# Output product of a gated slot attention layer: from two exact float32 pairs to twelve products of rounded halves, and two TensorE steps moved

## The reference, cut to what matters

```python
q = short_conv(h @ Wq, cq); k = short_conv(h @ Wk, ck); v = short_conv(h @ Wv, cv)
w = l2norm(short_conv(h @ Ww, cv)); g = log_sigmoid(h @ Wf1 @ Wf2); beta = sigmoid(h @ Wb)
# per token: Sk = Sk * exp(g) + k (beta w)^T;  Sv = Sv * exp(g) + (beta w) v^T
#            a = softmax(q Sk * SCALE);        o = a Sv
gate = h @ Wg1 @ Wg2 + bg2
o = o * rsqrt(mean(o * o) + EPS) * norm_w * sigmoid(gate)
attention = o.reshape(...) @ Wo
```

## Time and profile before

| | |
|---|---|
| median of 3 runs | 2137.21 us (2136.2 to 2137.25) |
| the profiled execution's own time | 2138.05 us |
| its span in the trace | 2136.1 us |
| mean granted clock of PE, as a share of full speed | 0.975 |
| PE / DVE / POOL / ACT busy | 92% / 82% / 67% / 66% |
| HBM traffic | 8 GB/s over the span |

### The profile page before, as it was taken

How to read it: one execution, slowest core, us unless ns; L and a number is a source line. 1 busy time by engine, 2 the same in 40 slices (tenths; PEclk the granted TensorE clock), 3 DMA queues, 4 the chain that set the end, 5 groups by cost and what they waited for, 6 DMA issues and landing times.

```text
span 2136.1 us, 41666 instructions
## 1 busy us (share of the span) xinstructions
PE 1961.0 (92%) x12064; PEld 1609.5 (75%) x12064; DVE 1750.6 (82%) x4091; ACT 1401.1 (66%) x3935; POOL 1430.1 (67%) x2461
## 2 busy tenths in 40 slices
PE   7799999999999999999999999999999999997676
PEld 6578777777778787777777787877777777775565
DVE  1788888888888888888888888888888888883555
ACT  2566777767767767777677777677776776773332
POOL 4367676777777776767777777767677777765233
PEclk8899999999999999999999999999999999998798
DMA  2000000000000000000000000000000000000000
GB/s 62 11 2 1 16 2 14 3 15 3 15 3 15 3 2 16 2 15 2 15 3 15 2 15 3 1 16 1 15 3 15 3 15 3 5 1 7 11 20 20
DMA packets 41737, 20.68 MB, mean 10 GB/s; under 512 B 13745, under 2 KB 41521, under 8 KB 41521
## 3 DMA queue, kind: packets, MB, share of 16 engines
q1 hardware_dynamic: 41520, 18.10, 3.1%
HBM read 15.99 MB, written 2.10 MB: 8 GB/s over the span
## 4 chain that ended last, share of the span: by engine, by line
PE 70%; DVE 12%; issue 8%; POOL 7%; ACT 2%; DMA 1%; DVEq 0%; SPq 0%; POOLq 0%; ACTq 0%
PE proj_ps L609 15%; PE mix_ps L693 11%; PE V_ps L664 8%; PE work_ps L721 7%; PE work_ps L727 6%; PE tr_ps L633 4%; DVE conv L479 4%; PE V_ps L642 3%; PE proj_ps L1281 3%; PE mix_ps L700 2%; PE work_ps L713 2%; DVE A L602 2%; PE proj_ps L1312 2%; POOL fused_lo L879 2%; DVE U L461 2%
## 5 line engine op out<-in xcount | busy, mean ns | idle before, releaser
L479 DVE SCALAR_TENSOR_TENSOR conv<-proj_ps,coefs,conv 128x511 f32<-128x511 f32 (+2 forms) x768 | 563.4, 734 | 11.3 <-ACT conv L334 4.3
L300 POOL TENSOR_TENSOR W<-W,tot 128x256 f32<-128x256 f32 x384 | 273.1, 711 | 200.1 <-PE mix_ps L693 200.1
L693 PE MATMUL mix_ps<-W,U 128*128 128x128 f32 x1792 | 299.9, 289 | 54.0 <-DVE A L602 41.4
L828 POOL TENSOR_TENSOR A_lev<-A,masks 128x256 f32<-128x256 f32 x448 | 322.9, 721 | 10.7 <-ACT A L377 10.7
L693 PEld LDWEIGHTS mix_ps<-W,U 128*128 128x128 f32 x1792 | 256.0, 191 | 91.4 <-DVE A L597 52.8
L664 PE MATMUL V_ps<-A_lev,UT 128*128 128x128 f32 x1792 | 284.2, 281 | 26.0 <-DVE V_ps L574 25.9
L602 DVE COPY_PREDICATED A<-masks,mix_ps 128x256 f32<-128x256 uint32 x448 | 268.2, 599 | 8.7 <-PE mix_ps L693 8.7
L664 PEld LDWEIGHTS V_ps<-A_lev,UT 128*128 128x128 f32 x1792 | 235.6, 191 | 51.5 <-DVE V_ps L574 51.3
L472 DVE TENSOR_TENSOR wT<-wT,tot 128x128 f32<-128x128 f32 x768 | 223.1, 331 | 41.9 <-DVE U L461 1.4
L574 DVE TENSOR_TENSOR V_ps<-V_ps,tot 128x256 f32<-128x256 f32 x384 | 164.9, 429 | 91.5 <-PE V_ps L664 91.2
L609 PE MATMUL proj_ps<-hT_hi,w_hi 128*128 128x512 f32 x512 | 223.1, 436 | 8.7 <-DVE conv L479 7.4
(11 more groups left out here) (175 smaller groups left out, 4738.5 us busy)
## 6 DMA issues: line engine op xcount, KB each, us to landing
acc<-in_L_attn_hidden_states SPq DMA_DIRECT2D x1, 2048.0 KB, 8.6
w_raw<-in_L_attn_Ww SPq DMA_DIRECT2D x16, 128.0 KB, 2.3
w_raw<-in_L_attn_Wq SPq DMA_DIRECT2D x16, 128.0 KB, 2.4
w_raw<-in_L_attn_Wk SPq DMA_DIRECT2D x16, 128.0 KB, 2.4
w_raw<-in_L_attn_Wv SPq DMA_DIRECT2D x16, 128.0 KB, 2.4
wo_raw<-in_L_attn_Wo SPq DMA_DIRECT2D x16, 128.0 KB, 2.2
out_x<-acc SPq DMA_DIRECT2D x4, 512.0 KB, 2.9
wf_head<-in_L_attn_Wf SPq DMA_DIRECT2D x16, 64.0 KB, 1.9
```

Source lines behind the costliest of these rows:

```text
L300: nc.gpsimd.tensor_tensor(w, w, block_tot(u3.par, lev, 0), ALU.mult).then_inc(W_step, 1)
L479: nc.vector.scalar_tensor_tensor(y_, proj_ps[:, CONV_BANK[i], 0:T - back], filt(u, i, KW - 1 - back), y_, ALU.mult, ALU.add).then_inc(conv ...
L693: last = nc.tensor.matmul(mix_ps[:, half, p * P:(p + 1) * P], Ulev(u3, lev)[:, p * P:(p + 1) * P], after_odd(W[:, p * T // 2:(p + 1) * T / ...
L828: nc.gpsimd.tensor_tensor(dst, diag_after_odd(lev), mask_cols(lev), ALU.mult)\
```

## The change

1. The output product is made from rounded halves. `og_hi` is `tg` rounded to the float32r form, `og_lo` the remainder, and `wo_hi` and `wo_lo` the same of `wo`. Three products per chunk (hi·hi, lo·hi, hi·lo) replace one float32 product: twelve instructions of 256 columns, all behind V's level r = 6, in place of two at r = 5 and two at r = 6.
2. The halves are made on ACT (`og_hi` at the end of r = 4 in each slot; `wo_hi` behind `wo`, once per head) and on POOL (`og_lo` at i = 5 in each slot; `wo_lo` at i = 3, once per head).
3. The gate product moves from the slot's end to r = 5 on PE. The last mixing product moves from r = 5 to behind level 6.
4. The attention output moves from between V's levels 7 and 8 to behind level 8; on ACT its copy `oN` moves behind V's copy and the tanh.

```diff
+                    if u4 and u4.par == 0 and i == 3:
+                        pool.wait_ge(wo_high, u4.h + 1)
+                        wait(pool, y_ps_ready, u4.count(2, 0))
+                        nc.gpsimd.tensor_tensor(wo_lo[:, :], wo[:, :], wo_hi[:, :].bitcast(F32), ALU.subtract)\
+                            .then_inc(wo_low, 1)
+                    if u4 and i == 5:
+                        pool.wait_ge(og_high, u4.count(1, 1))
+                        wait(pool, y_ps_ready, u4.count(2, 0))
+                        nc.gpsimd.tensor_tensor(og_lo[:, :], tg[:, :], og_hi[:, :].bitcast(F32), ALU.subtract)\
+                            .then_inc(og_low, 1)
...
+                        act.wait_ge(wo_scaled, u4.h + 1)
+                        nc.scalar.activation(wo_hi[:, :], wo[:, :], ACT.Copy).then_inc(wo_high, 1)
                     if u1 and r == 4:
                         tanh(act, u1, 1)
+                    if u4 and r == 4:
+                        act.wait_ge(og_done, u4.count(1, 1))
+                        nc.scalar.activation(og_hi[:, :], tg[:, :], ACT.Copy).then_inc(og_high, 1)
...
-                    if u4 and r in (5, 6):
-                        if r == 5:
-                            pe.wait_ge(og_done, u4.count(1, 1))
-                            pe.wait_ge(wo_scaled, u4.h + 1)
...
-                            last = mm(work_ps[:, r - 5, c * HID:(c + 1) * HID], tg[:, t0:t0 + P], wo[:, :],
-                                      start=True, stop=True)
...
+                    if u3 and r == 5:
+                        pe.wait_ge(head_g, 16 * (u3.h + 1))
...
+                        mm(proj_ps[:, 0, :], wg2_head[:, :], g1T[:, u3.par * T:(u3.par + 1) * T], start=True, stop=True)\
+                            .then_inc(gate_ps_ready, 1)
+                    if u3 and r == IN_CHUNK - 1:
+                        mix_products(pe, u3, r)
+                    if u4 and r == 6:
+                        pe.wait_ge(wo_low, u4.h + 1)
+                        pe.wait_ge(og_low, u4.count(1, 1))
...
+                            for n, (og, w) in enumerate(((og_hi, wo_hi), (og_lo, wo_hi), (og_hi, wo_lo))):
+                                last = mm(dst, og[:, rows], w[:, :], start=(n == 0), stop=(n == 2))
```

More of the change, by code:

```diff
@@ L126, in build @@
         wo = sb("wo", [P, HID])
+        wo_hi = sb("wo_hi", [P, HID], F32R)
+        wo_lo = sb("wo_lo", [P, HID], F32R)
         wf2_head = sb("wf2_head", [P, P])
@@ L159, in build @@
         tg = sb("tg", [P, T])
+        og_hi = sb("og_hi", [P, T], F32R)
+        og_lo = sb("og_lo", [P, T], F32R)
         y_sb = sb("y_sb", [P, C, HID])
@@ L193, in build @@
         names = ("x_in w_in small_in flip_ready head_w head_f head_g head_q head_k head_v head_o const_ready mask_ready xT_ps xT_hi xT_lo "
-                 "setup_hi setup_lo first_ps first_sb beta_step norm_set wo_scaled high_done low_done gbias_set "
+                 "setup_hi setup_lo first_ps first_sb beta_step norm_set wo_scaled wo_high wo_low og_high og_low high_done low_done gbias_set "
                  "proj_ps_ready gate_ps_ready wT_ps_ready vT_ps_ready A_ps_ready UT_ps_ready V_ps_ready KV_ps_ready s_ps_ready "
@@ L201, in build @@
         (x_in, w_in, small_in, flip_ready, head_w, head_f, head_g, head_q, head_k, head_v, head_o, const_ready, mask_ready, xT_ps,
-         xT_hi, xT_lo, setup_hi, setup_lo, first_ps, first_sb, beta_step, norm_set, wo_scaled, high_done, low_done,
+         xT_hi, xT_lo, setup_hi, setup_lo, first_ps, first_sb, beta_step, norm_set, wo_scaled, wo_high, wo_low, og_high, og_low, high_done, low_done,
          gbias_set,
@@ L990, in _ @@
                         nc.scalar.activation(Sv[:, u2.par % 2, 0, :], tr_ps[:, 0:P], ACT.Copy).then_inc(KV_done, 1)
-                if u3:
-                    act.wait_ge(o_ps_ready, u3.count(1, 1))
-                    wait(act, onT_ps_ready, u3.count(1, 0))
-                    nc.scalar.activation(oN[:, :], work_ps[:, 0, :], ACT.Copy).then_inc(oN_done, 1)
                 if u2:
@@ L1001, in _ @@
                     tanh(act, u1, 2)
+                if u3:
+                    act.wait_ge(o_ps_ready, u3.count(1, 1))
+                    wait(act, onT_ps_ready, u3.count(1, 0))
+                    nc.scalar.activation(oN[:, :], work_ps[:, 0, :], ACT.Copy).then_inc(oN_done, 1)
             act.wait_ge(ffn["q_in"], 48)
@@ L1282, in _ @@
                                          stop=True).then_inc(proj_ps_ready, 1)
-                    if u4 and r in (5, 6):
-                        if r == 5:
-                            pe.wait_ge(og_done, u4.count(1, 1))
-                            pe.wait_ge(wo_scaled, u4.h + 1)
-                            if u1:
-                                pe.wait_ge(wN_step, u1.count(4, 4))
-                        for c in range(2):
-                            t0 = (2 * (r - 5) + c) * P
-                            last = mm(work_ps[:, r - 5, c * HID:(c + 1) * HID], tg[:, t0:t0 + P], wo[:, :],
-                                      start=True, stop=True)
-                        last.then_inc(y_ps_ready, 1)
@@ L1295, in _ @@
-                    if u3 and r == IN_CHUNK - 2:
-                        mix_products(pe, u3, r + 1)
+                    if u3 and r == 5:
+                        pe.wait_ge(head_g, 16 * (u3.h + 1))
+                        if u1:
+                            pe.wait_ge(conv_step, u1.count(12, 6))
+                        elif u4:
+                            pe.wait_ge(tg_done, u4.count(1, 1))
+                        mm(proj_ps[:, 0, :], wg2_head[:, :], g1T[:, u3.par * T:(u3.par + 1) * T], start=True, stop=True)\
+                            .then_inc(gate_ps_ready, 1)
@@ new lines, in _ @@
+                    if u3 and r == IN_CHUNK - 1:
[3 more added lines that the diff above has]
+                        pe.wait_ge(og_low, u4.count(1, 1))
+                        if u1:
+                            pe.wait_ge(wN_step, u1.count(4, 4))
+                        for c in range(C):
+                            rows = slice(c * P, (c + 1) * P)
+                            dst = work_ps[:, c // 2, (c % 2) * HID:(c % 2 + 1) * HID]
+                            for n, (og, w) in enumerate(((og_hi, wo_hi), (og_lo, wo_hi), (og_hi, wo_lo))):
+                                last = mm(dst, og[:, rows], w[:, :], start=(n == 0), stop=(n == 2))
+                            if c % 2:
+                                last.then_inc(y_ps_ready, 1)
@@ L1312, in _ @@
-                    mm(proj_ps[:, 0, :], wg2_head[:, :], g1T[:, u3.par * T:(u3.par + 1) * T], start=True, stop=True)\
-                        .then_inc(gate_ps_ready, 1)
+                        pe.wait_ge(wN_step, u1.count(4, 4))
+                    if u4:
+                        pe.wait_ge(ys_done, u4.count(4, 2))
+                    outputs(pe, u3)
                 if u2:
```

10 lines of the change are left out of this document (removed).

## The result

| | before | after |
|---|---|---|
| median of the runs side by side | 2137.23 us (4 runs, 2136.2 to 2139.33) | 2230.86 us (4 runs, 2230.21 to 2231.8) |
| ratio, with its 95% interval | | 1.0437 (1.042 to 1.0453) |
| span of the profiled execution | 2136.1 us | 2228.2 us |
| mean granted clock of PE | 0.975 | 0.975 |
| ordinary slot, between two transposes of aN | 29.15 us | 30.15 us |

45 ordinary slots of +1.00 and 16 head slots of +3.00 make 45 + 48 = 93 us. The medians differ by 93.6, the spans by 92.1. ("Ordinary" in this table and in the next is the slot just ahead of a head slot; the three ordinary slots between two head slots are not all alike, see the experiments.) The granted clock is the same, so it has no part in this.

A forecast was written before the change was run, and what follows sets the result against it. It took DVE, held by POOL's reading instructions, to decide the slot rather than PE's own work. 45 ordinary slots x 1.25 = 56, 16 head slots x 3.0 = 48, and 4 gave +108, 2246 us; 8-in-10 range 2160 to 2285.

The forecast's parts named there:

- The first lock: Ordinary slot: POOL's og_lo holds DVE's pair in wT, DVE 1.5 us late at level 7, +0.8 us per slot.
- Rival (a): POOL's new work doesn't hold DVE; head slots still pay 2.0 us each; +29 us, 2167 us; chance 0.13.
- The second lock: DVE's growth of level 3 starts 0.1 us behind POOL's qk; slot +0.8, +1.25 or +1.7 us, middle taken.
- The sum of an ordinary slot: Ordinary slot, both meetings of DVE with POOL counted: +1.25 us, with ends 0.8 and 1.7.
- what the slot would be without POOL's work: Ordinary slot were DVE not held at all: bounded by aN, with 0.15 us to gain.
- The form's gain on PE: Output product on PE: twelve products at 0.119 us make 1.42 us against 1.72, saving 0.30 us per slot.
- ACT's og_hi: On ACT before the copy of UT: 0.62 us, hidden in 1.17 us of idle time, at nothing.
- The head slot: Each of 16 head slots: wo_lo's wait, late og_lo and weight split, 1.25 + 1.2 + 0.6 = 3.0 us; ends 2.0, 3.8.
- the last part: Head slot: POOL's split of the next head's weights meets DVE 2 us later, one or two more turns lost; 0.6 us.
- The end: Last three slots: og_hi and og_lo stand bare, nothing beside the output product; 4 us together.
- The total: Whole kernel: +108 us on 2138.05 us, 2246 us; own range 2216 to 2280, chance 0.65.
- Rival (b): Faster: PE is the bound, 0.30 us per slot comes out over 64 slots; -19 us, 2119 us; chance 0.12.

The follow-up runs named there:

- e7: Changed kernel with DVE's pair of products in wT issued one step later, behind the masked copy of r = 7; og_lo whole: 2187.39 us.
- e1: Changed kernel with og_lo made for 4 of its 512 columns only, the rest zeroed once at the start: 2150.35 us.
- e4: Kernel before with the moves alone, float32 output product in one piece at r = 6, no hi and lo parts: 2123.21 us, ratio 0.9926.
- e8: Changed kernel with og_lo of 4 columns and wo_lo moved from i = 3 to i = 5: 2124.99 us, ratio 0.9939.
- e3: Changed kernel with only wo_lo moved, from i = 3 to i = 5 in POOL's loop: 2209.69 us.
- e5: Kernel before with the halves and twelve products at r = 6, but gate product, mixing product and attention output at old places: 2257.08 us.
- e2: Changed kernel with a POOL fill of 1408 columns, which reads nothing, in place of og_lo: 2264.18 us.
- e9: Changed kernel with og_lo replaced by a 4-column reading subtraction, then a fill of 1280 columns, on POOL: 2199.93 us.

## Why the prediction was right, point by point

**The first lock** was the main step, and it held. Expected was the pair with about 2 us and DVE late by 1.5 at level 7; measured are 1.80 and 1.37. e7 shows the cause by moving the pair alone, and e1 by shortening og_lo. Rival (a), that POOL doesn't hold DVE, fell at once. e7 also shows a share that was no part of the lock: 0.38 us of the slot is PE's wait for og_lo, which in the changed kernel is hidden behind DVE's delay, as the prediction had it.

**The second lock** was a question of 0.1 us, and I had taken the middle of three outcomes: one turn lost. The pair takes 1.03, not 0.49, and starts at 1358.48, ahead of qk at 1358.56: its first product got through and the second waited. DVE was late by 1.26 there (26.91 us behind the transpose, against 25.65) and not by 1.5, which decided who was first. The lost turn cost 0.54 (1.03 less 0.49), for 0.45. The forecast itself called this a choice between three outcomes that the rows could not tell apart, so that the middle one came is luck, not a reading.

**The sum of an ordinary slot** is +1.00 for 1.25. The term that was mis-sized is what the slot would be without POOL's work. I put the gain there at 0.15; e1, e4 and e8 put it at 0.44 on average (28.76 for 29.20), and at 0.64 in the best slot. What I missed is what the moves give by themselves. From there og_lo adds 1.42 on average (30.18 less 28.77), where I had 1.4 from 29.0. So the cost was priced right and the gain too low.

**The form's gain on PE** is 0.22, not 0.30. I had priced twelve products at the 0.119 us of the earlier trace rows; from 1352.51 to 1353.90 the eleven distances are 0.126 each on average, since the first of them is 0.19 (1352.51 to 1352.70). It didn't matter, since the gain isn't on the path (e8 against e4).

**ACT's og_hi** was put at nothing. In the changed kernel the copy of UT that follows still has idle time in front of it:

```profile
1349.11 0.61 ACT L998 ACTIVATE og_hi<-tg 128x512 fp32r<-128x512 f32 x1
...
1350.37 0.38 ACT L396 ACTIVATE UT<-tr_ps 128x256 f32<-128x256 f32 x1 [0.65 <-PE tr_ps L637]
```

1.17 us of idle time became 0.65, and stays idle.

**The head slot** is +3.0 for +3.0, but that the sum came out is in part luck. Of its steps these stand: POOL's wait of 2.3 (2.31), PE's wait of 0.95 (0.96), and PE idle for the output product until og_lo is done. V's levels behind it come later than in an ordinary slot by 1.67 us, where I had 1.2 (DVE's decay for level 8 at 1387.27 is 25.56 behind the transpose of aN, against 23.89 there). My parts were 1.25 + 1.2 + 0.6. The first of them, the lock of an ordinary slot, does not happen in a head slot: the pair is over before og_lo begins, and e7 takes off only 0.1. What the runs give is 0.9 for og_lo's duration in front of the output product (e1), 1.73 for wo_lo's place once og_lo is narrow (31.85 in e1 less 30.12 in e8; 1.54 with the whole og_lo, e3), and 0.37 for the rest, of which 0.27 are there in e4, without any halves. So two parts were too large, one too small, and the total right.

I had put the last part down to the split of the next head's weights. A pair of 1.93 us at 1389.41, beside w_lo, is in the trace:

```profile
1389.06 2.13 POOL L364 TENSOR_TENSOR w_lo<-w_raw,w_hi 128x512 fp32r<-128x512 f32 x2
...
1389.41 1.93 DVE L476 TENSOR_TENSOR wT<-wT,tot 128x128 f32<-128x128 f32 x2
```

But the same meeting takes 2.09 us in e4, so it is not what the halves added. What speaks for the split is that the last head slot, the one without it, is 0.55 us shorter in e4 than before (28.43 for 28.98), where the others are 0.27 longer. That slot differs in other things too, and no run took the split away, so this part is argued, not shown.

**The end** was to cost 4 us. From the last transpose of aN to the end of the span it is 191.1 us before (1945.05 to 2136.1) and 192.8 after: +1.7. The first transpose of aN comes 1.0 us earlier (99.47 for 100.49), but that is within its scatter over the traces (99.5 to 103.1). The measured term is 1.7, and the sum by slots, 93, already covers the 92.1 between the spans without it.

**The total** was 2246 for 2230.9. The difference of 15 us is the ordinary slots' 45 x 0.25 = 11, and the rest is the end's 4, of which 2 or less is seen. One slip in the sum: the lower end of its range has 2.4 for a head slot, where the paragraph on the head slot gives 2.0; it changes nothing here. Rival (b), faster, is what e4 and e8 show: it needed POOL's work to be out of the way, and even then the gain came from the moves, not from the form. At 0.7% it is smaller than the 19 us that the rival had for the form alone.

## What to carry to other kernels

POOL's idle time can be in use by another engine: before giving POOL work in a gap, look at which of DVE's two-input operations run in exactly that gap. 33% idle on the page said nothing of this; two time lines side by side said it. And where an edit has two parts, one that shortens a product and one that moves it, time them apart: here the moves alone took off 15.6 us (e4 against its own runs of before) and the form, in one piece but without the other moves, added 118 (e5). A sum that comes out can hide parts that don't, as the head slot did: check each term against a run of its own.

## What the runs showed of the hardware that I had not expected

- DVE and POOL take turns instruction by instruction, and POOL hardly pays. Two DVE products of 0.49 us together took 1.80 beside og_lo and W, 1.03 beside the first part of qk, 1.93 beside w_lo; og_lo to W took 1.28 with and without a waiting product. The first half of this stood in the earlier trace rows; that it would split a pair whose first product starts 0.1 us ahead of POOL (1358.48 against 1358.56) I hadn't expected.
- The turn isn't kept against every POOL instruction. A waiting DVE copy was passed over by a fill (2.00 us, e2), where a reading instruction behind the same masked level let it in (0.80, in the changed kernel and in e9, where that instruction had 4 columns).
- A fill doesn't hold DVE's two-input products at all: 0.49 us beside 1.16 (e9). It did hold the copy, which has one input (e2). The same page of the Trainium skill, same section, has both kinds of DVE operation in one rule, and says that whoever starts first gets the ports; it doesn't say who is next, which is what decided the microsecond here.
